# The keys of an attention stage read from a second, transposed layout of the context, and split into bf16 parts by ScalarE and GpSimd in place of TensorE

## What is computed

```python
x = x + xattn(layernorm(x), ctx, ctx)     # 16 heads, d_k = 16
x = x + ffn(layernorm(x), w_gate, w_up, w_down)

# xattn
scores = einsum('bhqd,bhkd->bhqk', q, k) / 4
out = einsum('bhqk,bhkd->bhqd', softmax(scores), v)

# ffn: rows of x, h and the weights rounded to blocks of 16 of FP4 with a scale
h = silu(xq @ wq_gate.T) * (xq @ wq_up.T)
return hq @ wq_down.T
```

## Time and profile before

| | us |
|---|---|
| three runs | 579.61, 577.09, 580.11 |
| median | 579.61 |
| the profiled execution's own time | 575.73 |
| its span, first to last instruction | 573.9 |
| TensorE busy | 519.9 (91%) |
| VectorE busy | 452.0 (79%) |
| ScalarE busy | 364.3 (63%) |
| GpSimd busy | 270.3 (47%) |

### The profile page before, as it was taken

The page is one execution under the profiler, slowest core; times in us unless marked ns, Lnnn a source line. Parts: engine busy times, 40 slices in busy tenths (PEclk is TensorE's granted clock), DMA queues, the critical chain, the costliest instruction groups (busy, mean ns, idle before and its releaser), DMA issues.

```text
span 573.9 us, 13914 instructions
## 1 busy us (share of the span) xinstructions
PE 519.9 (91%) x4105; PEld 384.4 (67%) x4132; DVE 452.0 (79%) x1169; ACT 364.3 (63%) x704; POOL 270.3 (47%) x389
## 2 busy tenths in 40 slices
PE   2288999999999999999986789999999999999995
PEld 1134555555555555555543789999999999999994
DVE  1288888898988889898755588888888888898762
ACT  2224877877878778787786365556665555555642
POOL 3133334434344444343222466666666666666541
PEclk9999999999999999999998799999999999999999
DMA  7925454454454444423000000000000000000000
GB/s 224 232 65 150 120 140 121 124 147 121 121 147 118 127 116 138 135 80 98 4 3 0 2 10 17 14 18 18 18 18 18 18 18 18 9 18 19 19 20 27
DMA packets 43799, 40.63 MB, mean 71 GB/s; under 512 B 4728, under 2 KB 43512, under 8 KB 43768
## 3 DMA queue, kind: packets, MB, share of 16 engines
q1 hardware_dynamic: 43768, 40.26, 25.3%
HBM read 10.55 MB, written 4.19 MB: 26 GB/s over the span
## 4 chain that ended last, share of the span: by engine, by line
PE 79%; issue 5%; ACT 5%; DVE 4%; DMA 2%; POOL 2%; SPq 2%; another core or an unknown queue 0%; POOLq 0%; ACTq 0%; DVEq 0%
PE SC L958 20%; PE PV L958 12%; PE PV L912 12%; PE SC L880 10%; PE MX L894 9%; PE T L978 4%; PE T L822 3%; PE T L866 3%; PE T L983 2%; ACT KP L468 2%; PE T L829 2%; DVE MF L588 2%; ACT P L477 1%; DMA QS<-QP 1%; SPq L278 1%
## 5 line engine op out<-in xcount | busy, mean ns | idle before, releaser
L588 DVE TENSOR_REDUCE MF<-MX 128x2 f32<-128x512 f32 x256 | 170.1, 687 | 34.4 <-PE MX L894 31.6
L477 ACT ACTIVATE P<-SC 128x512 f32<-128x512 f32 x256 | 147.7, 599 | 45.4 <-PE SC L880 43.5
L894 PE MATMUL MX<-KS,QS 96*128 96x256 bf16 x512 | 104.3, 288 | 9.1 <-DMA QS<-QP 5.0
L880 PE MATMUL SC<-QS,KS 98*128 98x256 bf16 x512 | 99.2, 276 | 0.9 <-ACT P L477 0.5
L912 PE MATMUL PV<-P,VA 128*32 128x256 f32 x1024 | 82.5, 395 | 3.5
L880 PEld LDWEIGHTS SC<-QS,KS 98*128 98x128 bf16 x512 | 39.0, 98 | 58.5 <-ACT P L477 31.9
L426 POOL TENSOR_TENSOR HQ<-HN,hscale 128x704 f32<-128x704 f32 x32 | 44.6, 1394 | 66.4 <-DVE HN L741 66.4
L524 ACT ACTIVATE HH<-T 128x768 fp32r<-128x768 f32 x32 | 26.1, 814 | 77.9 <-PE T L978 77.9
L958 PE MATMUL SC<-WH,XH 128*128 128x352 f32 x256 | 68.0, 347 | 0.5 <-ACT XL L552 0.5
L894 PEld LDWEIGHTS MX<-KS,QS 96*128 96x128 bf16 x512 | 47.3, 100 | 30.5 <-DVE MF L588 18.0
L958 PE MATMUL SC<-WH,XL 128*128 128x352 f32 x256 | 62.4, 325 | 0.0
(11 more groups left out here) (109 smaller groups left out, 1015.8 us busy)
## 6 DMA issues: line engine op xcount, KB each, us to landing
KS<-KP SPq DMA_DIRECT2D x96, 128.0 KB, 2.4
QS<-QP SPq DMA_DIRECT2D x96, 128.0 KB, 2.5
X<-in_x SPq DMA_DIRECT2D x16, 256.0 KB, 2.8
C<-in_ctx SPq DMA_DIRECT2D x16, 256.0 KB, 3.0
out<-OB SPq DMA_DIRECT2D x32, 128.0 KB, 1.7
W<-in_L_ffn_w_down SPq DMA_DIRECT2D x1, 704.0 KB, 8.2
W<-in_L_ffn_w_gate SPq DMA_DIRECT2D x1, 640.0 KB, 5.2
W<-in_L_ffn_w_up SPq DMA_DIRECT2D x1, 640.0 KB, 6.3
```

The source lines that it names most:

```text
L477: nc.scalar.activation(P[g % 2][:, j, :, :], SC[h % 3][:, :, :], ACT.Exp, scale=0.25).then_inc(exp_done, 1)
L588: nc.vector.tensor_reduce(MF[st.slot(off, 2)][:, :, h:h + 1], MX[h % 2][:, :, :], AX.X, ALU.max, negate=True).then_inc(mx_done, 1)
L880: last = nc.tensor.matmul(SC[h % 3][:, k, :], KS[r][0:ROWS, h, k * 128:(k + 1) * 128], QS[r][0:ROWS, h, :], start=True, stop=True)
L894: last = nc.tensor.matmul(MX[h % 2][:, q, :], QS[r][0:PROD, h, q * 128:(q + 1) * 128], KS[r][0:PROD, h, :], start=True, stop=True)
```

## The change

The kernel gets the context a second time, as an input `ctx_t` laid out on the host: for each item 128 rows (a column of a head and a pair of heads) of 512 numbers (parity of the head, position). SP loads it into `KT`, 256 KB for each item, as a third transfer of every load. From it the three parts are made in SBUF: ScalarE writes part 0; GpSimd subtracts it from `KT` into `KR`; ScalarE writes part 1 from `KR`; GpSimd subtracts that from `KR` and writes part 2. The first subtraction is the first thing in GpSimd's step, the second stands behind rstd. GpSimd's two key copies, TensorE's flip and rests of the keys and their waits are gone, and so is ScalarE's third copy.

```diff
@@ sync: load
                 sp.dma_start(C[r][:, :, :], c_d[:, bass.ds(b * QT, QT), :]).then_inc(loaded[r], 16)
+                sp.dma_start(KT[r][:, :], t_d[:, bass.ds(b, 1), :].rearrange("p a c -> p (a c)")).then_inc(loaded[r], 16)
@@ gpsimd: attention_step
                 if st.has(LEAD):
                     r, rc = st.slot(LEAD, 2), st.slot(LEAD, RING)
-                    pool.wait_ge(loaded[rc], st.turn(LEAD, RING, 32))
-                    pool.wait_ge(k_tr, st.times(LEAD, 3))
+                    pool.wait_ge(k_out, st.times(LEAD, 3, 1))
                     gate(pool)
-                    for q in range(QT):
-                        nc.gpsimd.tensor_scalar(KN[:, q, :, :, :], by_parity(C[rc][:, q, :]), 1.0, 0.0,
-                                                ALU.mult, ALU.add).then_inc(kn_ready, 1)
+                    nc.gpsimd.tensor_tensor(KR[:, :], KT[rc][:, :], KP[r][:, 0, :], ALU.subtract).then_inc(k_rest, 1)
...
                     nc.gpsimd.tensor_tensor(rstd[r][:, :], ve[r][:, :], mhalf[:, :], ALU.pow).then_inc(rstd_ready, 1)
+                    pool.wait_ge(k_out, st.times(LEAD, 3, 2))
+                    gate(pool)
+                    nc.gpsimd.tensor_tensor(KP[r][:, 2, :], KR[:, :], KP[r][:, 1, :], ALU.subtract).then_inc(k_out, 1)
@@ scalar
+            def key_part(st, n):
+
+                r, rc, rs = st.slot(LEAD, 2), st.slot(LEAD, RING), st.slot(LEAD - 2, RING)
+                if n == 0:
+                    act.wait_ge(loaded[rc], st.turn(LEAD, RING, 48))
+                    if st.first + LEAD >= 2:
+                        act.wait_ge(stacked[rs], st.turn(LEAD - 2, RING, 192))
+                    nc.scalar.activation(KP[r][:, 0, :], KT[rc][:, :], ACT.Copy).then_inc(k_out, 1)
+                else:
+                    act.wait_ge(k_rest, st.times(LEAD, 1, 1))
+                    nc.scalar.activation(KP[r][:, 1, :], KR[:, :], ACT.Copy).then_inc(k_out, 1)
...
-                        for n, at in enumerate(((0, 1), (1, 0), (1, 2))):
+                        for n, at in enumerate(((0, 1), (1, 0))):
                             if (g, j) == at and st.has(LEAD):
-                                part_out(KP[st.slot(LEAD, 2)], TA, n, k_tr, k_out, st)
+                                key_part(st, n)
@@ tensor
-            def keys(st, n):
-                if n == 0:
-                    pe.wait_ge(kn_ready, st.times(LEAD, QT, QT))
-                    pe.wait_ge(o_norm, st.times(-1, 2))
-                    flip(TA, KN).then_inc(k_tr, 1)
-                else:
-                    pe.wait_ge(k_out, st.times(LEAD, 3, n))
-                    rest(TA, KP[st.slot(LEAD, 2)][:, n - 1, :], n == 2).then_inc(k_tr, 1)
...
             def maxima(st):
                 pe.wait_ge(m_parts, st.times(1, 1, 1))
-                pe.wait_ge(k_out, st.times(LEAD, 3, 3) if st.has(LEAD) else 3 * B)
...
-                        for n, at in enumerate(((0, 0), (0, 3), (1, 1))):
-                            if (g, j) == at and st.has(LEAD):
-                                keys(st, n)
@@ kernel
+    ctx = inputs["ctx_1024"].reshape(B, S, H // 2, 2, DK)
+    laid_out = dict(inputs, ctx_t=ctx.transpose(0, 4, 2, 3, 1).reshape(B, DK * H // 2, 2 * S))
```

More of the change, by code:

```diff
@@ L87, in ffn_steps, with program @@
     steps(eng, body, 0, 5, (TILES - 10) // 2, 2, TILES + 3, TILES)
-def program(nc, x, ctx_in, wg_in, wu_in, wd_in, out):
+def program(nc, x, ctx_in, ctx_t, wg_in, wu_in, wd_in, out):
     x_d = x.rearrange("b (q p) c -> p (b q) c", p=128)
     c_d = ctx_in.rearrange("b (q p) c -> p (b q) c", p=128)
+    t_d = ctx_t.rearrange("b p c -> p b c")
     o_d = out.rearrange("b (q p) c -> p (b q) c", p=128)
@@ L121, in program @@
         QN = sb("QN", [128, QT, 2, DK, H // 2])
-        KN = sb("KN", [128, QT, 2, DK, H // 2])
+        KT = [sb(f"KT{r}", [128, 512]) for r in range(RING)]
+        KR = sb("KR", [128, 512])
         KP = [sb(f"KP{r}", [128, 3, 512], bf16) for r in range(2)]
@@ L194, in program @@
         ve_ready, rstd_ready, qn_ready = sem("ve_ready"), sem("rstd_ready"), sem("qn_ready")
-        stats_seq, var_ready, kn_ready, neg_ready = (sem(n) for n in ("stats_seq", "var_ready", "kn_ready", "neg_ready"))
-        k_tr, q_tr, m_tr, o_tr = sem("k_tr"), sem("q_tr"), sem("m_tr"), sem("o_tr")
+        stats_seq, var_ready, k_rest, neg_ready = (sem(n) for n in ("stats_seq", "var_ready", "k_rest", "neg_ready"))
+        q_tr, m_tr, o_tr = sem("q_tr"), sem("m_tr"), sem("o_tr")
         k_out, q_out = sem("k_out"), sem("q_out")
@@ L384, in attention_step @@
                     nc.gpsimd.tensor_tensor(rstd[r][:, :], ve[r][:, :], mhalf[:, :], ALU.pow).then_inc(rstd_ready, 1)
+                    pool.wait_ge(k_out, st.times(LEAD, 3, 2))
+                    gate(pool)
+                    nc.gpsimd.tensor_tensor(KP[r][:, 2, :], KR[:, :], KP[r][:, 1, :], ALU.subtract).then_inc(k_out, 1)
                 if st.has(1):
                     r, rc = st.slot(1, 2), st.slot(1, RING)
-                    pool.wait_ge(loaded[rc], st.turn(1, RING, 32))
+                    pool.wait_ge(loaded[rc], st.turn(1, RING, 48))
                     pool.wait_ge(pv_done, st.times(0, NG))
@@ L593, in statistics @@
                 b, rc = st.item(LEAD), st.slot(LEAD, RING)
-                dve.wait_ge(loaded[rc], st.turn(LEAD, RING, 32))
+                dve.wait_ge(loaded[rc], st.turn(LEAD, RING, 48))
                 for q in range(QT):
@@ L1042, in _ @@
             ffn_steps(pe, ffn_step)
-_INS = ["x", "ctx_1024", "L0_ffn_w_gate", "L0_ffn_w_up", "L0_ffn_w_down"]
+_INS = ["x", "ctx_1024", "ctx_t", "L0_ffn_w_gate", "L0_ffn_w_up", "L0_ffn_w_down"]
 def kernel(**inputs):
@@ L1054 @@
     arrays, args = {}, []
+    ctx = inputs["ctx_1024"].reshape(B, S, H // 2, 2, DK)
+    laid_out = dict(inputs, ctx_t=ctx.transpose(0, 4, 2, 3, 1).reshape(B, DK * H // 2, 2 * S))
     for name in _INS:
-        a = np.ascontiguousarray(inputs[name])
+        a = np.ascontiguousarray(laid_out[name])
         arrays[f"in_{name}"] = a
```

## The result

The changed kernel takes **619.21 us** in the median of six runs (608.67 to 627.2), against 578.41 for the kernel before on the same chip (576.39 to 580.2). The ratio is **1.058, 95% interval 1.054 to 1.063**. The forecast was slower, 588.7, with a range from 577 to about 594. The direction was right; the size was not: 9.1 us were foretold and 32 came, 40 in the profiled execution.

A forecast was written before the change was run, and what follows sets the result against it. It took the attention loop of engines handing work on as the bound, closing through late rstd, normalisation and TensorE. Start +3.2 - 1.0, steps 0 and 1 -1.0, eleven steps +7.9: +9.1, median 588.7, range 577 to about 594.

The forecast's parts named there:

- the 17.29 worked out: Attention steps 2 to 12: late query flip at 7.34 plus 9.95 makes a step 17.29 against 16.57, +0.72 each.
- The extra 0.35 after the flip: Head 9's maxima product waits for VectorE's reduction of head 7, lengthening TensorE's stretch after the query flip from 9.60 to 9.95.
- Rival 1: rstd in time for the normalisation, TensorE's saving returns in all 13 steps: -4.3 us, 575.3, faster; chance 0.22.
- rival 2: GpSimd's subtraction takes only 0.62 us, the loop is 16.65: +2.1 us, 581.7, no change; chance 0.16.
- the second runs behind rstd and before VA ... no cost: GpSimd's second subtraction, 1.26 us, adds nothing, as VA is needed only a step later and GpSimd then idles.
- rival 3: Second subtraction blocks VectorE's normalisation: about 1.2 us more in 13 steps, +15.6 on top of +9.1, 604; chance 0.04.
- No hold: GpSimd does not hold VectorE's normalisation, read from a pair taking 0.91 beside VA and 0.90 without GpSimd work.
- The rule that I weighed: GpSimd and VectorE share an exclusive port pair, needed by VectorE only in 2-port mode or with two SBUF inputs.
- stood out waiting: TensorE, ready at about +6.2, spends all its freed time waiting for the query flip at +7.34.
- -0.5 each: Steps 0 and 1 have no residual adds, so rstd is in time and a step takes 16.07: -1.0 together.
- +2.2 foretold: Start: third loads queued ahead of the stacks, +3.2 at 324 GB/s, less 1.0 saved in steps -2 and -1.
- the 1.0 us that TensorE was to save in the steps before step 0: Steps -2 and -1 lose the key flip and a TensorE wait for a key copy: -1.0, bounds 0 and -2.

The follow-up runs named there:

- the first experiment: Changed kernel with GpSimd's second subtraction moved behind VA and made to wait for the normalised queries; median 600.83 us, ratio 1.036.

## Why the prediction was right or wrong

**What held.** The limit in the loop is the normalisation's start, and the forecast had it to 0.03 us (+6.36 for +6.39), by the right chain: ScalarE's key part at +1.80 (foretold +1.90), the subtraction at +2.61 (+2.71), two adds 1.41 (1.40), rstd. That the adds behind the first subtraction decide is shown by their exchange, which alone took 26 us off (33 between the profiled executions). But the 0.03 flatters: rstd ended at +6.23, 0.16 earlier than foretold, and the normalisation began 0.13 behind it, for which the sum had nothing. The subtraction was estimated at 1.26 and took 1.16; ScalarE's copy at 0.61 and took 0.63. The loads cost nothing in the loop. The step with the second subtraction out of the way and the clock up is 17.34, close to the 17.29 worked out, and that is luck: it has 0.30 of VA's hold in it, which the sum did not have, and 9.65 after the flip in place of 9.95. The extra 0.35 after the flip was nearly absent. Rival 1 (rstd in time) and rival 2 (the subtraction cheap) are out.

**First step that failed: "the second runs behind rstd and before VA ... no cost".** The normalisation starts when rstd is done, and so does the second subtraction; the first normalisation is held by the subtraction (0.74 lost), the second by VA, which follows (0.30 lost), and the pair takes 1.93, not 0.90. Since rstd is late already, all of it goes into the loop: normalisation at 6.36, pair 1.93, to TensorE 0.13, and 9.65 after the flip make 18.07, the measured step. That is rival 3, which I gave 0.04. It had the price at 1.2 a step, near the 1.03 that came, but put it all down to the subtraction.

The evidence against it was misread. VA ends at 170.47 and the normalisation begins at 170.28: they lie beside each other for 0.19 us at most. In all traces of this study the normalisations of over 0.52 us, 200 of them, ended 0.22 to 0.25 behind the recorded end of a GpSimd instruction; as one takes 0.48 by itself, the hold was over some 0.25 before that record was. By that, one that starts 0.19 before the recorded end meets nothing, and the pair's 0.91 against 0.90 can show neither a hold nor its absence. In the first experiment the normalisation begins 0.04 behind VA (262.35 and 262.31), and there it takes 0.80. "No hold" was read from a case that hardly overlapped.

The rule that I weighed was the right one. The rows show that the normalisation, whose one tensor input and output are both in SBUF, is held by each GpSimd instruction of 512 columns that began before it and ran on beside it, of one input or of two, on the same buffers or on others, until shortly before its recorded end. The Trainium skill, SBUF — State Buffer, section "SBUF: two separate sides", has the pair of ports go for a whole instruction to whoever starts first, and VectorE need it in a 2-port mode; and VectorE: DVE Perf Modes, section "What auto-detection actually checks", has VectorE take that mode where a single source and the destination are in SBUF and their outermost dimensions other than one are both even or equal. By that second page, the runs agree, the normalisation is such an instruction. I let a row decide what form it has; the form could have been read from the code.

**Second step that failed: TensorE "stood out waiting" at the price of the wait.** A stand-still was entered in the sum by its length. But 2.3 us of it is what TensorE did before its clock fell to 0.50, and for 3.4 or 6.8 us after it every product was slower. That is 1.5 or 3.0 us in eight of eleven steps, 16.8 in all in the profiled execution by the run with the filler products: nearly as much as all that the loop loses with the clock up, and absent from the forecast, its rivals and its range. Even with rival 3 the sum would have been +24.7 (604), and in the profiled execution +40.1 came: short by 15.4, about what the clock takes.

What stays open is why the clock falls after one wait and not after another. In steps 2 to 12 of the kernels tried, waits of about 0.84 came without a fall, and waits of 1.5 to 1.65, of about 1.9 and of about 2.3 with one in eight or nine of eleven steps. But a wait of 1.02 in step 1 of the kernel with the adds first had a fall behind it, and one of 1.07 in step 1 of the changed kernel had none.

**Third, steps 0 and 1:** -0.5 each was foretold, +1.6 and +0.6 came. There are no adds in them, but the hold is there just as well (pairs of 1.82 and 2.16, before 0.91), and in the run with filler products each is 1.1 above before.

**Fourth, the start:** +2.2 foretold, +4.55 measured, within the bounds. By the delay, the loads cost what they would at 215 to 230 GB/s and not at 324: the row of the time with loads alone was the wrong one, and that of the time with stacks, 204, the nearer. And of the 1.0 us that TensorE was to save in the steps before step 0 nothing came: from the first maxima product to the abs of step 0 it is 23.05 us in both kernels.

By its own steps: 2.2 - 1.0 + 7.9 = 9.1 was foretold. With the start at 4.55 (which has the -1.0 in it), the loop at full clock at 18.4, the clock at 16.8 and 0.4 for the rest it is 40.1, the profiled execution's.

## What to carry to other kernels

Where an instruction of VectorE from SBUF to SBUF and one of GpSimd can start at the same signal, put the one that is on the critical path alone: order GpSimd's work so that what nobody waits for comes after it, and put no new wait ahead of work that used to run early. Look at the single instructions, not at their sum: the pair's loss of 1.02 looked like one hold and was two. A row shows that two engines don't hold each other only if they overlap for longer than the hold could be. And price a new wait of TensorE's not by its length alone: if it is repeated in each step, look at the granted clock behind it, and try cheap products in the gap.

## What the runs showed of the hardware that was not expected

- After a stand-still of 2.27 us the granted clock was 0.50 from 178 to about 184.8, in the middle of a stage where TensorE is busy for over four fifths of the time; after one of 2.35 in another step it stayed at 1.00. Nine useless products of 2.10 us in all took a kernel from 610.8 to 599.3 us.
- VectorE's normalisation of 256 columns took 0.48 us free and up to 1.45 us beside one instruction of GpSimd, and a small operation of 18 columns took 0.16 and, beside VA, 0.63. Not everything of VectorE's was held: in the step shown the last three reductions from PSUM ahead of the normalisation take 1.89 us, with GpSimd busy all the time.
- GpSimd's subtraction of 512 columns with a bf16 operand and an fp32 one took 1.16 us, and with the same fp32 buffer as both operands 1.04.
